# Three quarters of the last wavelength's exponential on VectorE, in 20 of 32 units, and sums over wavelengths on TensorE

## The reference

```python
def wl_step(acc, wl):
    cpm, iw = wl
    m = cpm[None, :, None, None]
    scores = jnp.einsum('bhqd,bhkd->bhqk', Q * m, K * m) * SCALE
    scores = scores * jnp.cos(KERR * scores * scores)
    attn = jax.nn.softmax(scores, axis=-1)
    out = jnp.einsum('bhqk,bhkd->bhqd', attn, V)
    return (acc + out * iw, None)
```

## Time and profile before

| | us |
|---|---|
| median of 3 runs | 1883.58 (1883.06 to 1883.99) |
| profiled execution, its own time | 1883.32 |
| its span, first to last instruction | 1881.6 |
| ScalarE busy | 1818.4 (97%) |
| TensorE busy (products; weight loads beside them) | 1381.2 (73%); 836.5 |
| VectorE busy | 774.9 (41%) |
| GpSimd busy | 458.9 (24%) |
| mean granted clock of TensorE, of full speed | 0.987 |

### The profile page before, as it was taken

One profiled execution on the slowest core, in us unless ns is written; L12 is line 12 of the kernel. 1 busy time (PEld: TensorE's weight loads), 2 busy tenths in 40 slices (PEclk: granted clock), 3 DMA queues, 4 the chain that ended last, 5 costly groups with the idle time before them and its releaser, 6 DMA issues. The chain is left out here.

```text
span 1881.6 us, 42847 instructions
## 1 busy us (share of the span) xinstructions
PE 1381.2 (73%) x18990; PEld 836.5 (44%) x18990; DVE 774.9 (41%) x1452; ACT 1818.4 (97%) x553; POOL 458.9 (24%) x513
## 2 busy tenths in 40 slices
PE   4787787676688888888886667767667676666765
PEld 2354454443455555555554444444344444444444
DVE  7445564333345444444433334333333333333222
ACT  3799999999999999999999999999999999999995
POOL 6222233232122122112122245433212112212111
PEclk8799999999999999999999999999999999999998
DMA  6000110000201111101000000000000000000001
GB/s 203 16 14 15 57 37 31 26 20 14 50 7 38 41 41 41 41 10 33 21 21 14 20 23 13 23 24 16 14 14 2 14 14 14 14 14 2 7 13 30
DMA packets 44985, 49.89 MB, mean 27 GB/s; under 512 B 6725, under 2 KB 37359, under 8 KB 44799
## 3 DMA queue, kind: packets, MB, share of 16 engines
q1 hardware_dynamic: 42463, 42.91, 7.5%
q0 software_dynamic: 2048, 4.20, 0.8%
q10 hardware_dynamic: 288, 0.00, 0.0%
HBM read 30.96 MB, written 15.73 MB: 25 GB/s over the span
## 5 line engine op out<-in xcount | busy, mean ns | idle before, releaser
L933 ACT ACTIVATE Pr<-T 128x4096 f32<-128x4096 f32 x512 | 1796.2, 3636 | 1.3 <-DVE T L852 0.8
L894 PE MATMUL bank<-Pr,Vst 128*32 128x256 f32 x16384 | 992.5, 382 | 429.7 <-ACT Pr L933 264.5
L894 PEld LDWEIGHTS bank<-Pr,Vst 128*32 128x32 f32 x16384 | 575.1, 109 | 752.7 <-issue 569.4
L852 DVE COPY T<-bank 128x512 f32<-128x512 f32 x252 | 174.1, 691 | 482.4 <-PE bank L846 482.2
L939 POOL TENSOR_TENSOR gain<-rsum,iw_s 128x128 f32<-128x128 f32 x63 | 25.3, 402 | 1139.0 <-DVE rsum L925 1139.0
L836 DVE TENSOR_REDUCE negmax<-bank 128x2 f32<-128x512 f32 x256 | 165.0, 686 | 195.3 <-PE bank L830 194.8
L903 DVE COPY pv_s<-bank 128x512 f32<-128x512 f32 x192 | 131.3, 684 | 182.8 <-PE bank L894 182.7
L920 DVE COPY OT<-bank 128x432 f32<-128x432 f32 (+1 forms) x192 | 105.9, 552 | 118.4 <-PE bank L909 118.3
L909 PE MATMUL bank<-ident,pv_s 128*128 128x128 f32 x768 | 118.7, 277 | 24.3 <-DVE pv_s L903 24.3
L948 POOL TENSOR_TENSOR terms<-terms 128x512 f32<-128x512 f32 x126 | 128.1, 1017 | 9.9
L943 POOL TENSOR_TENSOR terms<-OT,gain 128x1024 f32<-128x1024 f32 x63 | 124.6, 1977 | 5.0
(11 more groups left out here) (168 smaller groups left out, 465.1 us busy)
## 6 DMA issues: line engine op xcount, KB each, us to landing
Ks<-qk_parts SPq DMA_DIRECT2D x31, 288.0 KB
Qs<-qk_parts SPq DMA_DIRECT2D x93, 96.0 KB
work<-in_L_ffn_w_dram SPq DMA_DIRECT2D x16, 256.0 KB, 3.9
qk_parts<-Pr SPq DMA_DIRECT2D x8, 384.0 KB, 2.8
qk_parts<-work SPq DMA_DIRECT2D x8, 384.0 KB, 3.1
dispatched<-T SPq DMA_DIRECT2D x5, 512.0 KB, 4.7
region<-dispatched SPq DMA_DIRECT2D x8, 320.0 KB, 3.9
expert_out<-work SPq DMA_DIRECT2D x8, 320.0 KB, 2.8
```

The lines of the kernel that those rows point to most:

```text
L852: nc.vector.tensor_copy(T[par][:, ds(p * BANK, BANK)], sc_bank[rr][:, :]).then_inc(sc_read, 1)
L894: ins = nc.tensor.matmul(bank[VC * j:VC * (j + 1), half * SEQ:(half + 1) * SEQ], Vst[par][:, at:at + VC], Pr[rr][:, blk * SEQ:(blk + 1) * ...
L933: nc.scalar.activation(Pr[rr][:, :], T[par][:, :], ACT.Exp, scale=scales[u % 2][w]).then_inc(exp_done, 1)
```

## The change

20 units, those of the PLAIN and FINAL pairs (`D_UNITS`), share the last wavelength (w = 15). Each 4096 columns are four blocks of 1024 (half and key tile); VectorE computes three of them into `d_out`, ScalarE the fourth (256 columns for each of 4 groups, one `activation` into `Pr_short`). VectorE has no exponential, so `dve_d_exp` makes one of seven operations: it scales by log2(e) x 2^23 and converts to an integer, cuts out mantissa and exponent by masks, and forms a polynomial of the mantissa as a product of two quadratics times the power of two. The 21 operations of a unit are spread over its steps by `D_OPS_AT`. In step 15 `pe_products` takes its moving operand from `d_out` for the first three blocks and from `Pr_short` for the fourth. The Pr buffers alternate over whole exponentials only (`buffer_of`).

In all units the end of the chain changes. `dve_turned` no longer copies to OT but takes reciprocals from the bank, multiplies by the weights and forms `terms` for the group, three operations. `pe_sum` adds them over wavelengths on TensorE, by products with the identity into `sum_bank` (which lies in the same bank as the target of `pe_turn_max`), two steps after the group's last wavelength (`SUM_AT`: w = 4, 7, 9, 12, 15, and w = 0 of the next unit). `dve_heads` copies the sum out at w = 1 of the next unit. GpSimd's `sum_half` goes. `pe_turn_max` and `dve_turn_max` move from the end of phase B to the end of step `MAX_AT` = 4, and the first sum of a unit waits for `nm_copied`. GpSimd stages V when the unit's products are done. At setup GpSimd makes `cd`, the scales for VectorE.

```diff
+    DCOLS = 4 * SEQ
+    DCHUNKS = 3
+    SHORT = (COLS // DCOLS - DCHUNKS) * SEQ
+    DOPS = 7
@@ setup, GpSimd
-                        nc.gpsimd.tensor_tensor(c_side, scaled, cosine, ALU.mult)
+                        ins = nc.gpsimd.tensor_tensor(c_side, scaled, cosine, ALU.mult)
+                    link(ins)
+                    nc.gpsimd.tensor_scalar(cd[:, :], cw[:, :].rearrange("p (u w) -> p u w", w=W)[:, :, W - 1], LOG2E * MANT, None, ALU.mult)
@@ pe_products
+                        if shared and c < DCHUNKS:
+                            pe.wait_ge(d_step, DOPS * (D_UNITS.index(u) * DCHUNKS + c + 1))
+                        if shared and c == DCHUNKS:
+                            pe.wait_ge(exp_done, u * W + w + 1)
@@
+            def dve_d_exp(dve, u, par, i):
+                c, op = divmod(i, DOPS)
...
+                if op == 0:
...
+                    ins = nc.vector.tensor_scalar(d_scaled[:, :].rearrange("p (j k) -> p j k", k=SEQ), src, cd[:, u:u + 1], FLOOR, ALU.mult, ALU.max)
+                elif op == 1:
+                    dve.wait_ge(d_step, made + 1)
+                    ins = nc.vector.tensor_scalar(d_mantissa[:, :].bitcast(i32), d_scaled[:, :], 0x007FFFFF, 0x3F800000,
+                                                  ALU.bitwise_and, ALU.bitwise_or)
+                elif op == 2:
+                    ins = nc.vector.tensor_scalar(d_scaled[:, :], d_scaled[:, :], 0x40000000, 0x7F800000,
+                                                  ALU.bitwise_xor, ALU.bitwise_and)
+                elif op == 3:
+                    dve.wait_ge(d_step, made + 2)
+                    ins = nc.vector.scalar_tensor_tensor(out_[:, :], d_mantissa[:, :], r1, d_mantissa[:, :], ALU.add, ALU.mult)
+                elif op == 4:
+                    ins = nc.vector.scalar_tensor_tensor(d_mantissa[:, :], d_mantissa[:, :], r2, d_mantissa[:, :], ALU.add, ALU.mult)
+                elif op == 5:
+                    dve.wait_ge(d_step, made + 4)
+                    ins = nc.vector.scalar_tensor_tensor(out_[:, :], out_[:, :], s1, d_scaled[:, :].bitcast(f32), ALU.add, ALU.mult)
+                else:
+                    dve.wait_ge(d_step, made + 6)
+                    ins = nc.vector.scalar_tensor_tensor(out_[:, :], d_mantissa[:, :], s2, out_[:, :], ALU.add, ALU.mult)
+                ins.then_inc(d_step, 1)
@@ dve_turned
-                nc.vector.tensor_copy(dst, src).then_inc(turned_copied, 1)
+                nc.vector.reciprocal(rsum[:, 0:size, :].unsqueeze(3), slots[:, :, :, HD:OC]).then_inc(inverted, 1)
+                dve.wait_ge(inverted, n + 1)
+                nc.vector.tensor_tensor(gain[:, 0:size, :], rsum[:, 0:size, :], weight, ALU.mult).then_inc(gain_ready, 1)
+                dve.wait_ge(gain_ready, n + 1)
...
+                nc.vector.tensor_tensor(terms[n % 2][:, 0:size, :].rearrange("p s (a d) -> p s a d", d=HD), slots[:, :, :, 0:HD],
+                                        gain[:, 0:size, :].unsqueeze(3).to_broadcast([P, size, OTW, HD]), ALU.mult).then_inc(terms_ready, 1)
+            def pe_sum(pe, u, q):
+                n = u * GROUPS + q
+                pe.wait_ge(terms_ready, n + 1)
+                if q == 0:
+                    pe.wait_ge(nm_copied, min(u + 2 if u else 1, UNITS - 1) + 2)
+                    if u:
+                        pe.wait_ge(summed, u)
+                for w in range(FIRST_OF[q], LAST_OF[q] + 1):
+                    ins = nc.tensor.matmul(sum_bank, ident[:, :], terms[n % 2][:, w - FIRST_OF[q], :], start=w == 0, stop=w == W - 1)
+                ins.then_inc(terms_summed, 1)
@@ act_step
+                if w == W - 1 and u in D_UNITS:
+                    act.wait_ge(pv_done, 2 + u * W)
+                    blocks = T[par][:, :].rearrange("p (j b) -> p j b", j=GR)[:, :, DCHUNKS * SEQ:]
+                    nc.scalar.activation(Pr_short[:, :, :], blocks, ACT.Exp, bias=LN_FACTOR if DCHUNKS % QT else 0.0, scale=scales[u % 2][w]).then_inc(exp_done, 1)
+                    return
@@
+            D_UNITS = [u for u in range(UNITS) if KINDS[u // 2] in (PLAIN, FINAL)]
+            D_OPS_AT = (2, 1, 2, 0, 2, 2, 1, 2, 0, 2, 2, 0, 3, 2, 0, 0)
+            MAX_AT = 4
@@ VectorE's step
                         if phase == B and one:
                             dve.wait_ge(exp_done, W * u + 1)
                             dve_transposed(dve, pair_no(u, 1, two), 1 - par, k, rr)
+                        if u in D_UNITS:
+                            for i in range(D_DONE[w], D_DONE[w + 1]):
+                                dve_d_exp(dve, u, par, i)
...
                         if w in TURN_AT:
                             dve_turned(dve, u, TURN_AT[w])
+                        if w == MAX_AT and two and not first:
+                            dve_turn_max(dve, pair + 1, par)
@@ TensorE's step
+                        if w == MAX_AT and two and not first:
+                            pe_turn_max(pe, u + 2, u)
+                        if w in SUM_AT:
+                            pe_sum(pe, u, SUM_AT[w])
```

More of the change, by code:

```diff
@@ L131, in attention_and_experts @@
         pv_s = [sb(f"pv_s{i}", [P, BANK]) for i in range(2)]
[L132 to L139, removed]
+        Pr_short = sb("Pr_short", [P, GR, SHORT])
+        d_scaled = sb("d_scaled", [P, DCOLS], i32)
+        d_mantissa = sb("d_mantissa", [P, DCOLS])
+        d_out = [sb(f"d_out{i}", [P, DCOLS]) for i in range(DCHUNKS)]
+        rsum = sb("rsum", [P, SLOTS, OTW])
+        gain = sb("gain", [P, SLOTS, OTW])
+        terms = [sb(f"terms{i}", [P, SLOTS, OTW * HD]) for i in range(2)]
+        mv = sb("mv", [P, TILES, 2])
+        ln = sb("ln", [P, 6, TILES])
         negmax = [sb(f"negmax{i}", [P, SIDE_TILES]) for i in range(2)]
@@ L912, in dve_turned @@
             def dve_turned(dve, u, q):
[L914 to L919, removed]
@@ L920, in dve_turned @@
-                nc.vector.tensor_copy(dst, src).then_inc(turned_copied, 1)
[L922 to L925, removed]
-            def load_scales(act, u):
-                act.reg_load(scales[u % 2], cw[0:1, u * W:(u + 1) * W].bitcast(i32))
@@ L931, in act_step @@
[L931 to L955, removed]
@@ L976, in attention_and_experts @@
             TURN_AT = {min(last + 1, W - 1): q for q, last in enumerate(LAST_OF)}
+            SUM_AT = {last + 2: q for q, last in enumerate(LAST_OF) if last + 2 < W}
             A, B, C, D_ = range(4)
@@ L1048, in step @@
                             pe_turn(pe, u, TURN_AT[w])
-                    def after(phase):
-                        if phase == (C if first else B) and two:
-                            pe_turn_max(pe, u + 2)
-                    run_steps(step, after, first)
+                        if w == MAX_AT and two and not first:
+                            pe_turn_max(pe, u + 2, u)
+                        if w in SUM_AT:
+                            pe_sum(pe, u, SUM_AT[w])
+                    run_steps(step, lambda phase: None, first)
                 units(unit)
+                pe_sum(pe, UNITS - 1, GROUPS - 1)
             def plain_vector(dve):
@@ L1080, in step @@
                             dve_products(dve, u, TURN_AT[w])
+                        if w == 1 and u:
+                            dve_heads(dve, u - 1)
+                        if w == 2 and u == 1:
+                            dve_turn_max(dve, 1, 0)
                         if phase == A and two:
@@ L1100, in after @@
                             dve_split(dve, pair_no(u, 0), u + 2, par)
-                        if phase is None:
-                            dve_row_sums(dve, u, 0)
-                        if phase == (C if first else B) and two:
-                            dve_turn_max(dve, pair + 1, par)
-                        if phase == C:
-                            dve_row_sums(dve, u, 1)
                     run_steps(step, after, first)
                 units(unit)
-                dve.wait_ge(pool_step, HALF_STEPS * (2 * UNITS - 1))
-                sum_half(dve, nc.vector, last_half, 0, UNITS - 1, 1)
+                dve_heads(dve, UNITS - 1)
                 dve.wait_ge(summed, UNITS)
@@ L1151, in plain_gpsimd, with unit @@
                     stage_v(pool, u, u)
-                def unit(u, par, last=False):
-                    for half in range(1 if last else 2):
-                        sum_half(pool, nc.gpsimd, pool_step, HALF_STEPS * (2 * u + half), u, half)
+                def unit(u):
+                    for half in range(2):
                         paced = u * W + WH * half + 10
@@ L1166, in plain_gpsimd @@
                 CU = EU + E + 1
-                for u in range(H):
-                    unit(u, u % 2)
+                for u in range(2 * LAST):
+                    unit(u)
                     stage_next(pool, u)
-                for u in range(H, 2 * LAST):
-                    unit(u, u % 2)
-                    stage_v(pool, u + 2, u % 2)
-                unit(UNITS - 2, 0)
-                unit(UNITS - 1, 1, last=True)
```

92 lines of the change are left out of this document (73 added, 19 removed).

## The result

The changed kernel takes 1928.66 us (median of 4 runs, 1928.11 to 1928.90), the kernel before 1883.45 (1883.06 to 1883.99): ratio 1.0239, 95% interval 1.0222 to 1.0257. It is slower by 45.2 us, where 25.7 were predicted. The profiled execution spans 1927.1 us (1881.6 before) at a mean granted clock of 0.967 (0.987).

A forecast was written before the change was run, and what follows sets the result against it. ScalarE's exponentials were taken to bound the kernel, filling 1796 of 1881.6 us. From 1883.3 us, -51.2 + 32.4 + 30.6 + 12.4 + 2.3 + 0.5 - 1.35 = +25.7 gave 1909 us; predicted range 1874 to 1922, the forecast's own 1893 to 1923.

The forecast's parts named there:

- Short exponential: ScalarE's 16th exponential in 20 units: step 0.95 us instead of 3.51, saving 51.2 us.
- Vector work: VectorE's added operations: 20.7 us a unit for the shared exponential; reciprocal, gain and terms 1.21 us with waits.
- The upper bound for masks: VectorE's masks over integers, 1024 columns: 0.70 to 1.23 us each, 0.70 taken.
- Hold at w = 4: TensorE waits at `nm_copied` behind VectorE's queued operations; exponential 7 stalls 1.8 us in 18 units, 32.4 us.
- Clock in the hole: TensorE's clock falls to half behind the w = 4 wait; products 5 end 1.7 us later in 18 units, 30.6 us.
- rival 1: TensorE's clock stays up in the w = 4 holes: 1878.4 us, a little faster; chance 0.17.
- the upper bound given: Clock price at w = 4 with the sum slow as well: 2.4 us in each of 18 units, 43 us.
- End of a unit: Steps w = 14, 15, 0: exponential 2 of the next unit stalls 0.65 us behind 19 units, 12.4 us.
- First pairs: Stalls of 0.4 and 0.9 us in the second pair, 1.0 in the first for side work; together 2.3 us.
- GpSimd's sums: End of the chain on GpSimd: its sums go, and nothing but the last unit waited for them.
- Range: The forecast's own range around 1909 us, 1893 to 1923, from clock price, end of a unit and masks.
- the four rivals: Clock stays up (0.17); that with single-rate masks (0.06); TensorE not held at w = 4 (0.06); ScalarE's step no shorter (0.02).

The follow-up runs named there:

- third experiment: The changed kernel with VectorE's copy of the maxima put before the two queued exponential operations of step 4: 1862.40 us, ratio 0.9886 to the kernel before.
- fourth experiment: The changed kernel with no unit sharing its exponential; summing on TensorE and moved maxima stay: 1885.97 us, ratio 1.0007 to the kernel before.
- sixth experiment: The fifth experiment's kernel with GpSimd's bias moved to units 10 to 13 and its other two combine operations each after a later exponential: 1835.87 us, ratio 0.9741.
- fifth experiment: The third experiment's kernel with the fifth group's sum moved from w = 15 to behind products 0 of the next unit: 1849.96 us, ratio 0.9819.
- first experiment: The changed kernel with GpSimd's three operations of each combine cut from 1024 to 64 columns: 1909.88 us, ratio 1.0144 to the kernel before.

## Why the prediction was wrong

The direction and the mechanism at w = 4 were right; the time was not (1909 us predicted, 1928.66 measured), because one term was missing: what GpSimd's combine does to VectorE's new operations.

- **Short exponential:** right. It takes 1.04 us and its step 0.945; 0.95 was taken.
- **Vector work:** right. A mask takes 0.69 us and two-tensor operations 1.22, where 0.70 and 1.2 were taken; reciprocals on 48 columns 451 ns for 453. The upper bound for masks wasn't needed, and "VectorE: DVE Perf Modes" of the Trainium skill, The perf-mode tier table, by which an fp32 tensor_scalar in SBUF runs at double rate, agrees with the 0.69 us of the masks, which are on integers. A small slip: reciprocal, gain and terms, put at "1.21 us" with their waits, add up to 1.22 without them; they took 1.28 in the kernel after (1292.33 to 1293.61).
- **Hold at w = 4:** right, 1.83 us for 1.8, in 18 units (2.17 in one of them), by the copy of the maxima behind two queued operations. The third experiment takes it away.
- **Clock in the hole:** right in kind and size, 28.6 us for 30.6. It fell in 16 of 18 holes, so rival 1 held in two units. In four units the whole sum and all products were slow (1.62 us instead of 0.91 and 3.64 instead of 1.93), 2.4 over the hold, the upper bound given.
- **End of a unit:** 0.69 us for 0.65. The mechanism is as worked out, and its own times give 0.69 (8.65 less 7.96); 0.65 was a slip, 0.8 us in all.
- **First pairs:** 4.0 for 2.3. The largest part is unit 1, 2.16 us where 1.0 was taken for the side work of the first pair; 1.4 of that is the clock, which the prediction looked for only in the 18 holes. The second pair took 0.98 twice, for 0.4 and 0.9.
- **GpSimd's sums, the step that failed:** "GpSimd's sums go; nothing but the last unit waited for them." True of what GpSimd loses, but the step asked only that and put the work that GpSimd keeps, the combine, at nothing. `dve_turned` was costed by its mean ("Gain on 48 columns 0.21", from a row, L741, with one of its inputs in a bank), and it gives VectorE an operation that reads SBUF twice in the middle of the chain to TensorE; the copy to OT that it replaces read a bank. And only w = 4 and the end of a unit were timed step by step: that the shared exponential moves `gain` from 0.14 to 1.10 us behind the start of exponential 8, onto the combine, was not seen. The fourth experiment has the `gain` and the combine without the shared exponential, the sixth has `gain` and shared exponential without the combine in that place; neither loses the 18.1 us. The combine was in the trace of before and harmless there, as these lines of its timeline show:

```profile
1105.09 1.90 POOL L763 TENSOR_TENSOR region<-region,r 128x1024 f32<-128x1024 f32 x1
...
1107.07 2.37 POOL L765 TENSOR_TENSOR base<-base,region 128x1024 f32<-128x1024 f32 x1
...
1107.50 0.69 DVE L852 COPY T<-bank 128x512 f32<-128x512 f32 x1 [2.17 <-PE bank L846]
1108.11 0.45 DVE L920 COPY OT<-bank 128x288 f32<-128x288 f32 x1
1108.59 0.95 DVE L925 RECIPROCAL rsum<-OT 128x128 f32<-128x128 f32 x1
```

VectorE's copies out of banks and its reciprocal with one input from SBUF run at their usual length beside it; an operation with two inputs from SBUF isn't there to be held, for `gain` was GpSimd's own. The combines cost 18.1 us in four units, and no bound covered that; with them the sum is +43.8, for +45.5 measured.
- **Range:** the widths named for it (clock price 18 to 37, end of a unit -6 to +6, masks +7) add up to 1890 to 1928 us, wider than the 1893 to 1923 stated, and none of them is for the combine.

None of the four rivals was this one. It would have been found by asking of each new VectorE operation not only who waits for it but what else, on GpSimd, runs beside it, and by how much the operations ahead of it move it.

## What to carry to other kernels

When an operation on a helper engine grows, look in its queue for short operations behind it that others wait for, and put those first: here a copy of 0.21 us behind 2.4 us of work cost 61.6 us, nearly half of it through TensorE's clock. A new VectorE operation with both inputs in SBUF is priced beside GpSimd's work of its unit, not by its mean. And a step on the critical engine is measured from start to start: a wait may hide 0.1 us in a lost overlap, where idle time shows nothing.

## What the hardware did that was not expected

- VectorE's operation with two SBUF inputs waits for whole operations of GpSimd, not for a share of the time: 0.21 us became 4.73 behind two of them, 1.61 and 1.00 behind the rest of one. A mask, with one SBUF input on 1024 columns, took 2.27 instead of 0.69. A copy out of a bank was untouched at 0.69. The Trainium skill, "GPSIMD Engine Reference", Specifications, says that the two engines share their SBUF interfaces, with contention for VectorE's instructions in a 2-port mode or with two SBUF inputs. The traces agree, and add that the wait lasts until GpSimd's operation ends. Why the held `gain` has a record that begins 0.44 us before GpSimd's first operation (0.59 in the fifth experiment) stays open.
- Three back-to-back operations of GpSimd can hold it across more than one: in three of the four units `gain` got its turn only after the second (at 1124.36), in the fourth after the first. What decides is open.
- Both sides may pay: GpSimd's copy of 128 columns, mean 0.295 us in the sixth experiment, had a mean of 0.423 in the kernel after, 1.29 us at 1126.66 beside a VectorE operation that itself took 2.34. In the fourth unit the third operation of the combine took 3.23 us instead of 2.36.
- TensorE's clock fell in 16 of 18 holes with a wait of 2.90 us (one 3.26). Why it held in two is open; no run here tells the two from the others. In unit 1 a wait of 2.33 us was followed by the low clock in the kernel after, and one of 2.34 wasn't in the first experiment; behind the 1.74 us of units 2 and 3 it never fell.
